# The three convolutions as 64-row by 32-column tiles of the PE array, the upper rows one piece ahead of the lower

## The chip, the core and the metric

The program runs on one core of a Trainium2 chip. The metric is the device time of one execution in microseconds (us). Three timed runs of the kernel before gave 4041.86 us as median (4040.77 to 4042.82). The engines are TensorE (PE, with its weight loads as PEld), VectorE (DVE), ScalarE (ACT), GpSimd (POOL) and SyncE (SP, here only a DMA queue).

## The reference

An image batch x of 64 x 16 channels x 128 x 128 goes through four layers, each "normalise in 8 groups of 2 channels, then transform, then add".

```python
x = x + L0(_gn(x), 5)      # Newton-Schulz inverse of each 128x128 plane, 5 iterations
x = x + L1(_gn(x), ...)    # quantised 3x3 convolution, 16 -> 16 channels, zero padding
x = x + L2(_gn(x), w)      # 5x5 convolution whose kernel is filter_w on its diagonal only
x = x + L3(_gn(x), w)      # 3x3 convolution with circular padding (given as FFTs)
```

The change touches the three convolutions L1, L2 and L3 alone.

## The kernel before

**Two stages.** The first computes layer 0 for all 64 images and ends at about 2274 us. The second runs the convolutions. An image lies in SBUF as 128 partitions = 8 image rows x 16 channels, and 16 blocks j of 8 image rows in the free dimension, each padded to 132 columns. A "piece" is 4 blocks of one image in one layer: one PSUM bank of 128 x 512. There are four pieces (u = 0 to 3) for each image and layer, and 6 banks go round among the pieces (`B_RING`).

**The matmuls of a piece.** Within a block, the 3x3 convolutions (layers 1 and 3) are three 128 x 128 matmuls of 512 columns, one for each horizontal tap, whose weights hold the vertical taps as bands. The image rows just outside a block (one above, one below) are copied by DMA into a tile `xh` of 96 partitions (`halo_copies`, six DMAs an image and layer), and one matmul more with `wth` adds them. Layer 1 has one product; layers 2 and 3 split data and weights into high and low f16 halves and take three products. So a piece of layer 1 has 4 matmuls and one of layer 3 has 12 (`conv`). For layer 2 the tile `xk` holds the image with each of its 8 image rows skewed by one more column (`skew_row`, eight DMAs an image), so that a tap on the diagonal is one fixed offset. `diagonals` uses weight tiles of 128 rows x 32 columns: four of them, at the four column strips of the array, read four different offsets. A product is 8 matmuls (two for each strip) and 4 for the rows outside the block, which only the first and last strip have: 36 a piece.

**The order of the work.** It is written out by hand, in steps s. A step holds layer 1 of image s, layer 2 of image s-1 and layer 3 of image s-3 on TensorE, and the normalisation of layers 2 (image s) and 3 (image s-2) on the other engines. TensorE's order in a step is four pieces of layer 1, `mean(3)`, layer 3 with `var(3)` after its first piece, `mean(2)` after its second and `var(2)` after its fourth, then four pieces of layer 2. `mean` and `var` are tiny f32 matmuls that sum statistics over partitions: `mean(l)` waits for VectorE's `whole_stats`, `var(l)` for its `deviations`, and VectorE's `variance` waits for `var`.

VectorE's order is: layer 1's four `residual`s (PSUM times scale plus the old image), each with the statistics for layer 2 (`chunk_stats`), `deviations(3)` before the fourth; `whole_stats(2)`, `variance(3)`, `clamp`, `normalise(3)`, `integers`; layer 3's four residuals with `deviations(2)`, `variance(2)` and `normalise(2)` between and behind them; layer 2's four residuals, each with statistics; `whole_stats(3)`.

ScalarE has `upper(l)` (two passes that scale the image, `F`, and round it to f16, `xn`), which waits for `normalise(l)`; POOL has `lower(l)`, the low f16 half in four instructions, which waits for `upper`. `wrap` on ScalarE writes layer 3's circular borders. SP issues the skews once `lower(2)` is done, the load of a later image, its share of the halo copies and the store of the result. ScalarE issues the other halo copies in its own queue.

## Time and profile before

| | |
|---|---|
| timed runs, median (lowest to highest) | 4041.86 us (4040.77 to 4042.82) |
| the profiled execution: its time, its span | 4042.99 us, 4041.2 us |
| mean granted clock of TensorE | 0.989 |
| busy: PE, PEld | 3882.1 us (96%), 2994.3 us (74%) |
| busy: DVE, ACT, POOL | 3161.3 us (78%), 2458.9 us (61%), 2416.6 us (60%) |
| instructions | 91064 |
| DMA, whole span | 422.11 MB, mean 104 GB/s |

The page is one profiled execution. Busy time is the union of an engine's instructions; matmuls are pipelined, so that each lasts longer in the record than it holds the array, and the distance between starts is the better measure of their price. "Idle before" is time in which the engine stood still ahead of a group, with what ended it behind the arrow. The granted clock is given as a share of 2.4 GHz: 1.00 is 2.4 GHz and 0.50 is 1.2 GHz. A DMA "lands" when its data are written and its semaphore is up.

### The profile page before, as it was taken

The page shows a single profiled execution, that of the slowest core. Times are in us where ns is not written, and L with a number is a line of the kernel's source. Part 1 is how long each engine was busy: PE and PEld are TensorE (multiplying, and loading weights), DVE is VectorE, ACT ScalarE, POOL GpSimd, SP SyncE. Part 2 cuts the span into 40 slices and gives each one's busy share as a digit, 9 for nine tenths or more (in the row PEclk, how much of TensorE's full clock was granted, in tenths as well). Part 3 has the DMA queues.
Part 4 walks back from the last instruction along what each step waited for, and adds up shares of the span by engine and source line. Part 5 has one row for each costly group of instructions (what it writes and reads, how often), then busy time and mean ns, then how long its engine had stood idle before and what let it go on. Part 6 is the DMA issues. An engine that isn't in the chain of part 4 may idle for free. (4 is left out here: it accounts for less than half of the span.)

```text
span 4041.2 us, 91064 instructions
## 1 busy us (share of the span) xinstructions
PE 3882.1 (96%) x35017; PEld 2994.3 (74%) x35017; DVE 3161.3 (78%) x7205; ACT 2458.9 (61%) x4490; POOL 2416.6 (60%) x3154
## 2 busy tenths in 40 slices
PE   7999999999999999999999589999999999999998
PEld 7999999999999999999999344444444444444443
DVE  5888888888888888888888667777777777777774
ACT  5776677777777777777777345455455455555552
POOL 6888888888888888888888323333332332332332
PEclk9999999999999999999999799999999999999999
DMA  2122211222122222221221368777777777778774
GB/s 71 56 63 64 64 59 59 64 64 59 58 64 64 64 64 64 64 64 56 61 64 43 75 133 175 174 165 162 164 168 175 169 160 163 169 171 175 162 159 106
DMA packets 339918, 422.11 MB, mean 104 GB/s; under 512 B 25312, under 2 KB 288160, under 8 KB 323104
## 3 DMA queue, kind: packets, MB, share of 16 engines
q1 hardware_dynamic: 324128, 377.40, 39.1%
q10 hardware_dynamic: 15360, 38.88, 3.7%
q8 instruction: 282, 4.62, 0.5%
q14 instruction: 148, 1.21, 0.1%
HBM read 135.18 MB, written 134.22 MB: 67 GB/s over the span
## 5 line engine op out<-in xcount | busy, mean ns | idle before, releaser
L1228 POOL TENSOR_TENSOR xn<-F,xn 128x512 f16<-128x512 f32 x512 | 543.4, 1093 | 1189.6 <-ACT xn L1270 1189.6
L1444 PE MATMUL bank<-xn,wt 128*128 128x512 f16 (+1 forms) x3072 | 765.0, 384 | 15.3 <-DVE xn L1314 11.8
L484 ACT ACTIVATE P<-bank 128x512 f32<-128x512 f32 x1024 | 606.6, 608 | 267.6 <-PE bank L1007 155.4
L1466 PE MATMUL bank<-xk,wt 128*32 128x512 f16 x6144 | 634.9, 386 | 43.3 <-DMA xk<-xn 42.9
L1328 DVE SCALAR_TENSOR_TENSOR x<-bank,wu,x 128x512 f32<-128x512 f32 x512 | 377.4, 747 | 299.7 <-PE bank L1471 269.9
L1444 PEld LDWEIGHTS bank<-xn,wt 128*128 128x128 f16 (+1 forms) x3072 | 296.0, 102 | 361.8 <-issue 40.1
L1267 ACT ACTIVATE F<-x,nb,r 128x2048 f32<-128x2048 f32 x128 | 268.1, 2095 | 346.6 <-issue 218.6
L1471 PE MATMUL bank<-xk,wth 128*32 128x512 f16 x3072 | 469.2, 381 | 0.0
L1466 PEld LDWEIGHTS bank<-xk,wt 128*32 128x32 f16 x6144 | 295.6, 95 | 204.9 <-DMA xk<-xn 47.6
L334 POOL TENSOR_TENSOR W<-W 128x512 f16<-128x512 f32 x256 | 289.5, 1160 | 145.1 <-ACT W L517 145.1
L1338 DVE BATCH_NORM_STATS2 bs<-x 128x6 f32<-128x512 f32 x512 | 355.5, 694 | 17.6
L597 DVE BATCH_NORM_STATS2 st<-X 128x6 f32<-128x256 f32 x1024 | 351.5, 409 | 5.8 <-DMA X<-in_x 5.7
L526 ACT ACTIVATE W<-X,nb,r 128x256 f32<-128x256 f32 x512 | 258.7, 587 | 133.8 <-POOL nb L362 130.4
L379 POOL TENSOR_TENSOR S<-P 128x512 f32<-128x512 f32 x256 | 317.8, 1278 | 33.5 <-ACT P L484 33.4
L390 POOL TENSOR_TENSOR P<-P,idt 128x512 f32<-128x512 f32 x256 | 318.3, 1272 | 31.4 <-ACT P L484 31.4
L374 POOL TENSOR_TENSOR YX<-idt,YX 128x512 f32<-128x512 f32 x256 | 323.7, 1275 | 5.5 <-ACT YX L474 5.5
L385 POOL TENSOR_TENSOR S<-S,P 128x512 f32<-128x512 f32 x256 | 318.5, 1277 | 0.0
L1449 PE MATMUL bank<-xh,wth 96*128 96x512 f16 (+1 forms) x1024 | 307.7, 381 | 7.4 <-DMA xh<-xn 7.4
L1471 PEld LDWEIGHTS bank<-xk,wth 128*32 128x32 f16 x3072 | 165.3, 96 | 171.2 <-issue 3.2
L474 ACT ACTIVATE YX<-bank,cs 128x128 f32<-128x128 f32 x1024 | 277.8, 382 | 11.3 <-PE bank L939 2.7
L701 DVE SCALAR_TENSOR_TENSOR X<-bank,cout,X 128x128 f32<-128x128 f32 x1024 | 270.5, 343 | 13.0 <-PE bank L1033 13.0
L635 DVE TENSOR_TENSOR P<-bank,idt 128x512 f32<-128x512 f32 x256 | 176.9, 691 | 109.1 <-PE bank L1024 103.4
(144 smaller groups left out, 8369.3 us busy)
## 6 DMA issues: line engine op xcount, KB each, us to landing
xk<-xn SPq DMA_DIRECT2D x512, 131.8 KB, 4.4
X<-in_x SPq DMA_DIRECT2D x64, 1024.0 KB, 4.8
x_scratch<-X SPq DMA_DIRECT2D x64, 1024.0 KB, 5.8
X<-x_scratch SPq DMA_DIRECT2D x64, 1024.0 KB, 8.6
out<-x SPq DMA_DIRECT2D x64, 1024.0 KB, 6.8
xh<-xn SPq DMA_DIRECT2D x192, 131.8 KB, 4.6
xh<-xn ACTq DMA_DIRECT2D x192, 131.8 KB, 5.5
xh<-xn SPq DMA_DIRECT2D x192, 65.9 KB, 5.2
```

The costliest lines, as they stand in the source:

```text
L374: nc.gpsimd.tensor_tensor(e, eyes, e, ALU.subtract).then_inc(a_new, 1)
L379: nc.gpsimd.tensor_tensor(quad(S, q), quad(P1, q), quad(P2, q), ALU.add).then_inc(s_new, 1)
L385: nc.gpsimd.tensor_tensor(quad(S, q), quad(S, q), quad(P3, q), ALU.add).then_inc(q_new, 1)
L390: nc.gpsimd.tensor_tensor(quad(P2, q), quad(P2, q), eyes, ALU.add).then_inc(r_new, 1)
L484: nc.scalar.activation(into[:, 4 * q:4 * q + 4, :], banks[q][:, :].rearrange("p (m w) -> p m w", m=4), ACT.Copy).then_inc(sb, 1)
L597: ins = nc.vector.bn_stats((st0, st1)[k][:, g, :], group_of(X[slot], g))
L1228: ins = nc.gpsimd.tensor_tensor(padded(xn[l][n % 2], 1)[:, a + 1:a + 5, L:L + H], F[l][:, a:a + 4, :], padded(xn[l][n % 2], 0)[:, a + 1:a ...
L1328: nc.vector.scalar_tensor_tensor(out=dst, in0=bank, scalar=col[:, 0:1], in1=xs_of(l, n)[:, at, :], op0=ALU.mult, op1=ALU.add).then_inc(eva ...
L1338: nc.vector.bn_stats(bst_[l][:, u, :], xs_of(l, n)[:, 4 * u:4 * u + 4, :]).then_inc(gchain[l], 1)
L1444: nc.tensor.matmul(bank, wt[l][:, a, k, :], v, start=(k == a == b == 0), stop=False)
L1466: nc.tensor.matmul(bank[32 * q:32 * q + 32, :], wt[2][:, a, e, 32 * q:32 * q + 32], rows(b, 2 * q + e, 0), start=(a == b == e == 0), stop= ...
L1471: ins = nc.tensor.matmul(bank[32 * q:32 * q + 32, :], wth[2][:, a, e, 32 * q:32 * q + 32], rows(b, 2 * q + e, back), start=False, stop=(a ...
```

## The change

**Tiles.** `conv` and `diagonals` are replaced by one function, `strips`. It issues, for one half of the array's rows (partitions 0 to 63, or 64 to 127) and one unit i of the piece (a product and a weight matrix), four matmuls with 64 x 32 weights, one for each column strip of 32. A piece is 3 units in layer 1, 6 in layer 2 and 9 in layer 3, each once for the upper and once for the lower half: 24, 48 and 72 matmuls of 512 columns.

**The rows outside a block.** In the upper half (image rows 0 to 3) the last strip, output rows 6 and 7 of a block, has no neighbour in its own block; it reads the next block instead, whose first row lies just below. In the lower half (image rows 4 to 7) the first strip, output rows 0 and 1, reads the previous block. `wth` now holds weights for these strips in the shape of `wt`. The tiles `xh`, the halo DMAs on SP and on ScalarE, and their semaphores are gone.

**Order.** The upper half of a piece is issued interleaved unit by unit with the lower half of an earlier piece (`piece`, `lower_strips`), so that the two halves write different banks at a time. The lower half of a piece starts after its upper half's last matmul (`upper_ps`), at the soonest two units into the next piece (`GAP`), and stays at most two pieces behind (`BEHIND`). `conv_ps`, for which VectorE waits, rises with the lower half's last matmul. `mean`, and `var` at two places, first bring the lower halves that they depend on up to date (`finish`). `var(2)` moves from after the fourth piece of layer 3 to after the first piece of layer 2.

**Queues.** ScalarE runs `root(2)` and `upper(2)` before `wrap`, instead of behind it and its DMAs. SP sends each skew as two: the high part as soon as `upper(2)` is done (`high`), the low part after `lower(2)` (`normed`): 16 DMAs of half the size, behind the load and the store of the step. At the start, 18 small weight DMAs stand for 8 earlier ones, and two more tiles are zeroed.

```diff
-                    def conv(l, n, u):
...
-                                nc.tensor.matmul(bank, wt[l][:, a, k, :], v, start=(k == a == b == 0), stop=False)
-                        if u == 0:
-                            pe.wait_ge(halo[l][n % 2], 16 * 6 * (n // 2 + 1))
...
+                    def strips(l, n, u, half, i):
+                        a, b = products[l][i // mats[l]]
+                        k = i % mats[l]
+                        if half == 0 and i == 0:
+                            if u == 0:
+                                ready(l, n)
+                            bank_free(l, n, u)
+                        bank = bank_of(l, n, u)
+                        part = slice(64 * half, 64 * half + 64)
+                        for q in range(4):
+                            back = {(1, 0): -1, (0, 3): 1}.get((half, q), 0)
+                            cols_ = slice(32 * q, 32 * q + 32)
+                            w = (wth if back else wt)[l][part, a, k, cols_]
+                            if l == 2:
+                                at = (4 * u + 1) * PW + L + SK - (2 * q + k) + back * (PW + RB)
+                                v = xk[n % 2][part, b, at:at + 4 * PW].rearrange("p (j w) -> p j w", w=PW)[:, :, 0:H]
+                            else:
+                                at = 4 * u + 1 + back
+                                v = padded(xn[l][n % 2], b)[part, at:at + 4, L + k - 1:L + k - 1 + H]
+                            ins = nc.tensor.matmul(bank[cols_, :], w, v, start=(half == i == 0),
+                                                   stop=(half == 1 and i == length[l] - 1))
+                        if half == 1 and i == length[l] - 1:
+                            ins.then_inc(conv_ps[l], 1)
+                        if half == 0 and i == length[l] - 1:
+                            ins.then_inc(upper_ps, 1)
...
                     def mean(l, n):
+                        finish(l - 1, n, BPI - 1)
...
+                    def lower_strips():
+                        k, i = below
+                        if i == 0:
+                            pe.wait_ge(upper_ps, k + 1)
+                        strips(*order[k], 1, i)
+                        below[:] = [k, i + 1] if i + 1 < length[order[k][0]] else [k + 1, 0]
+                    def piece(l, n, u):
+                        k = place[l, n, u]
+                        for i in range(length[l]):
+                            strips(l, n, u, 0, i)
+                            if below[0] < k - (i < GAP):
+                                lower_strips()
+                        while below[0] < k - BEHIND:
+                            lower_strips()
...
-                    sp.wait_ge(normed[1], 1)
-                    halo_copies(sp, 1, 0, False)
+                    def skew(n, part):
+                        for r in range(RB):
+                            at, to = PW + L, PW + L + SK - r
+                            sp.dma_start(xk[n % 2][C * r:C * r + C, part, to:to + RUN],
+                                         xn[2][n % 2][C * r:C * r + C, part, at:at + RUN]).then_inc(skewed[n % 2], 16)
...
-                            sp.wait_ge(wrapped, 2 * (s - 1))
-                            halo_copies(sp, 3, s - 2, False)
+                        if there(s):
+                            need(sp, conv_ps[2], BPI * (s - 1))
+                            sp.wait_ge(high[2], s + 1)
+                            skew(s, 0)
+                            sp.wait_ge(normed[2], s + 1)
+                            skew(s, 1)
```

**TensorE, the end of a step.** Before, from `mean(2)` on (`s,gm` and `q,gm` are the two statistics matmuls):

```order
L1478 MATMUL bank<-s,gm 128x1 [waits gvar_sb2,bst_done2]
L1444 MATMUL bank<-xn_1,wt 128x512 [waits evac1]
L1444 MATMUL bank<-xn_1,wt 128x512 x8
L1449 MATMUL bank<-xh_1,wth 128x512 x3
L1444 MATMUL bank<-xn_1,wt 128x512 [waits evac1]
L1444 MATMUL bank<-xn_1,wt 128x512 x8
L1449 MATMUL bank<-xh_1,wth 128x512 x3
L1483 MATMUL bank<-q,gm 128x1 [waits spread2]
L1466 MATMUL bank<-xk,wt 32x512 [waits evac1,halo2_1]
L1466 MATMUL bank<-xk,wt 32x512 x7
L1471 MATMUL bank<-xk,wth 32x512 x4
```

In the change, the first units of layer 2's first piece (`xk`, upper half) with those of layer 3's third piece (`xn_0`, lower half), where the wait for the skews now stands:

```order
L1445 MATMUL bank<-xk,wt 32x512 [waits evac1,skewed0]
L1445 MATMUL bank<-xk,wt 32x512 x2
L1445 MATMUL bank<-xk,wth 32x512
L1445 MATMUL bank<-xn_0,wth 32x512
L1445 MATMUL bank<-xn_0,wt 32x512 x3
L1445 MATMUL bank<-xk,wt 32x512 x3
L1445 MATMUL bank<-xk,wth 32x512
```

And the end of that piece:

```order
L1445 MATMUL bank<-xk,wt 32x512 x3
L1445 MATMUL bank<-xk,wth 32x512
L1445 MATMUL bank<-xn_0,wth 32x512
L1445 MATMUL bank<-xn_0,wt 32x512 x3
L1461 MATMUL bank<-q,gm 128x1 [waits spread2]
L1445 MATMUL bank<-xk,wt 32x512 [waits evac1]
```

The matmul for `var(2)` (`q,gm`) stood ahead of the first matmul that waits for the skews; it now stands behind six units that follow this wait, and so do the lower halves of layer 3's last pieces.

**ScalarE, from `root(2)` on.** Before (`sd` is the square root, `T` belongs to the next step):

```order
L1275 ACTIVATE sd<-ve 128x1 [waits gvar_sb2]
L1249 ACTIVATE xn_0<-xn_0 128x2x16 [waits normed3]
L1251 ACTIVATE xn_0<-xn_0 128x2x16
L1253 ACTIVATE xn_0<-xn_0 128x2x132 [waits wrap_chain]
L1254 ACTIVATE xn_0<-xn_0 128x2x132
L1184 DMA xh_0<-xn_0 16x2x2108 [waits wrapped]
L1184 DMA xh_0<-xn_0 16x2x2108 x2
L1267 ACTIVATE F<-x_0,nb,r 128x2048 [waits normed2,scale_set2]
L1270 ACTIVATE xn_0<-F 128x16x128 [waits scaled_f2]
```

In the change:

```order
L1265 ACTIVATE sd<-ve 128x1 [waits gvar_sb2]
L1257 ACTIVATE F<-x_0,nb,r 128x2048 [waits normed2,scale_set2]
L1260 ACTIVATE xn_0<-F 128x16x128 [waits scaled_f2]
L1239 ACTIVATE xn_0<-xn_0 128x2x16 [waits normed3]
L1241 ACTIVATE xn_0<-xn_0 128x2x16
L1243 ACTIVATE xn_0<-xn_0 128x2x132 [waits wrap_chain]
L1244 ACTIVATE xn_0<-xn_0 128x2x132
L1250 ACTIVATE T<-X,ncol,acol 128x2048 [waits normed1,x1_in0]
```

The two passes of `upper(2)` now stand right behind the square root; the wait for `normed3` and the DMAs that stood ahead of them are behind them or gone.

## Rows read from the trace of the kernel before

**Rows 1.** The page: busy time, share and instructions by engine; clock in 40 slices.

```profile
PE 3882.1 (96%) x35017; PEld 2994.3 (74%) x35017; DVE 3161.3 (78%) x7205; ACT 2458.9 (61%) x4490; POOL 2416.6 (60%) x3154
...
PEclk9999999999999999999999799999999999999999
```

**Rows 2.** Stretches, 3000 to 3500 us: busy time and instructions by engine, clock, DMA.

```profile
3000.00:3500.00 500.00, 481.81 (x4092) 229.85 (x4092) 376.40 (x871) 254.57 (x228) 159.55 (x151) 1.00 0.76 168
```

**Rows 3.** Groups by line, 2600 to 4000 us: count, busy, mean ns, idle before.

```profile
L1228 POOL TENSOR_TENSOR xn<-F,xn 128x512 f16<-128x512 f32 x424 | 448.4, 1089 | 950.4 <-ACT xn L1270 950.4
...
L1328 DVE SCALAR_TENSOR_TENSOR x<-bank,wu,x 128x512 f32<-128x512 f32 x424 | 312.4, 747 | 221.6 <-PE bank L1471 214.9 <-PE bank L1449 4.9
```

**Rows 4.** Timeline of TensorE in one step: start us, us, instructions.

```profile
3304.60 0.62 PE L1466 MATMUL bank<-xk,wt 128*32 128x512 f16 x8 [0.16 <-DMA xk<-xn]
...
3307.22 0.62 PE L1466 MATMUL bank<-xk,wt 128*32 128x512 f16 x6
...
3315.17 0.83 PE L1444 MATMUL bank<-xn,wt 128*128 128x512 bf16 x3
...
3316.06 0.82 PE L1444 MATMUL bank<-xn,wt 128*128 128x512 bf16 x3
...
3322.13 2.13 PE L1444 MATMUL bank<-xn,wt 128*128 128x512 f16 x9
...
3324.75 0.28 PE L1478 MATMUL bank<-s,gm 128*128 128x1 f32 x2
```

**Rows 5.** Timeline of 3304.60 to 3304.62 us, after TensorE's wait.

```profile
3304.60 0.11 PEld L1466 LDWEIGHTS bank<-xk,wt 128*32 128x32 f16 x6 [0.24 <-DMA xk<-xn]
3304.60 0.40 PE L1466 MATMUL bank<-xk,wt 128*32 128x512 f16 x4 [0.16 <-DMA xk<-xn]
```

**Rows 6.** Timeline of VectorE in one step.

```profile
3304.48 0.16 DVE L1364 TENSOR_SCALAR ve<-bank 128x1 f32<-128x1 f32 x1 [0.91 <-PE bank L1483]
...
3305.92 0.16 DVE L1372 RECIPROCAL ra<-sd 128x1 f32<-128x1 f32 x1 [0.62 <-ACT sd L1275]
...
3306.86 0.21 DVE L1381 TENSOR_SCALAR nb<-r,m 128x1 f32<-128x1 f32 x1
...
3316.87 0.75 DVE L1328 SCALAR_TENSOR_TENSOR x<-bank,sws,X 128x512 f32<-128x512 f32 x1
...
3318.26 0.73 DVE L1328 SCALAR_TENSOR_TENSOR x<-bank,sws,X 128x512 f32<-128x512 f32 x1
...
3321.02 0.14 DVE L1350 TENSOR_TENSOR dv<-bs,bank 128x8 f32<-128x8 f32 x1
...
3321.75 0.74 DVE L1328 SCALAR_TENSOR_TENSOR x<-bank,sws,X 128x512 f32<-128x512 f32 x1
```

**Rows 7.** The chain of waits in the same step: start us, us, what.

```profile
3313.06 2.10 ACT F L1267
...
3317.18 4.24 POOL xn L1228 x4
...
3321.43 0.59 SPq L1176
...
3326.19 5.11 DMA xk<-xn
...
3331.35 0.83 PE bank L1466 x8
```

**Rows 8.** Tile xk, 2600 to 4000 us: the DMAs' time to landing.

```profile
DMA to landing us min/median/max: 3.3/4.4/5.7
```

**Rows 9.** Timeline of TensorE near the end: a wait and what follows.

```profile
3977.86 0.38 PE L1478 MATMUL bank<-s,gm 128*128 128x1 f32 x2 [1.77 <-DVE s L1342]
3978.11 3.11 PE L1444 MATMUL bank<-xn,wt 128*128 128x512 f16 x9
```

**Rows 10.** Two stretches there: before the clock fell, and while it was down.

```profile
3974.00:3979.00 5.00, 3.23 (x33) 1.48 (x28) 3.25 (x8) 3.02 (x2) 1.87 (x2) 1.00 0.24 56
3979.10:3982.40 3.30, 3.30 (x11) 1.35 (x9) 1.36 (x3) 0.00 (x0) 2.26 (x3) 0.50 0.02 5
```

More of the change, by code:

```diff
@@ L136, in conv_net @@
         w_loaded = sem("w_loaded")
-        W_PIECES = 3 + 2 + len(HALO2)
+        W_PIECES = 3 + sum(len(edges[l]) for l in (1, 2, 3))
         w_top = sem("w_top")
@@ L1117, in conv_net @@
             T = sb("T", [H, NJ, H])
-            xh = [None] + [None if l == 2 else [sb(f"xh{l}_{n}", [6 * C, parts[l], NJ * PW], kinds[l]) for n in range(2)]
-                           for l in (1, 2, 3)]
             xk = [sb(f"xk{n}", [H, 2, SFLAT], f16) for n in range(2)]
@@ L1141, in conv_net @@
             wrap_chain = sem("wrap_chain")
-            halo = [None] + [[sem(f"halo{l}_{n}") for n in range(2)] for l in (1, 2, 3)]
-            skewed = halo[2]
+            skewed = [sem(f"skewed{n}") for n in range(2)]
             xk_zeroed = sem("xk_zeroed")
+            upper_ps = sem("upper_ps")
             conv_ps = [None] + [sem(f"conv_ps{l}") for l in (1, 2, 3)]
@@ L1154, in conv_net @@
             CH = 8
+            GAP = BEHIND = 2
             LATE = (None, 0, 1, 3)
@@ L1168, in conv_net @@
             place = {piece: k for k, piece in enumerate(order)}
+            products = (None, [(0, 0)], [(0, 0), (0, 1), (1, 0)], [(0, 0), (0, 1), (1, 0)])
+            length = [None] + [len(products[l]) * mats[l] for l in (1, 2, 3)]
             def bank_of(l, n, u):
                 return banks[place[l, n, u] % B_RING]
[L1173 to L1185 removed]
             with nc.Block() as block:
@@ L1296, in _ @@
                             root(2, s)
+                            upper(2, s)
                         if there(s - 2):
                             wrap(s - 2)
[L1299 to L1302 removed]
                 @block.vector
@@ L1484, in var, with finish @@
                                          stop=True).then_inc(gvar[l], 1)
+                    below = [0, 0]
+                    def lower_strips():
[12 more added lines that the diff above has]
+                            lower_strips()
+                    def finish(l, n, u):
+                        k = place[l, n, u]
+                        while below[0] <= k:
+                            lower_strips()
                     for s in range(STEPS):
-                        if there(s):
-                            for u in range(BPI):
-                                conv(1, s, u)
+                        for u in range(BPI):
+                            if there(s):
+                                piece(1, s, u)
                         if there(s - 2):
@@ L1493, in _ @@
                             if there(s - 3):
-                                conv(3, s - 3, u)
+                                piece(3, s - 3, u)
                             if there(s - 2) and u == 0:
+                                if there(s):
+                                    finish(1, s, BPI - 2)
                                 var(3, s - 2)
-                            if there(s):
-                                if u == 1:
-                                    mean(2, s)
-                                if u == 3:
-                                    var(2, s)
-                        if there(s - 1):
-                            for u in range(BPI):
-                                diagonals(s - 1, u)
+                            if there(s) and u == 1:
+                                mean(2, s)
+                        for u in range(BPI):
+                            if there(s - 1):
+                                piece(2, s - 1, u)
+                            if there(s) and u == 0:
+                                if there(s - 3):
+                                    finish(3, s - 3, 0)
+                                var(2, s)
+                    finish(*order[-1])
 def kernel(x, L1_conv_weight_int8, L1_conv_scale_weight, L1_conv_bias, L2_conv_filter_w, L3_conv_weight):
```

101 lines of the change are left out of this document (26 added, 75 removed).

## The prediction, made before the change was run

> **What bounds the kernel now.** First the page: TensorE is busy 96% of the span, and its clock is at full speed but for two places, the change of stage and the end [rows 1]. The change touches only the second stage. There the table of stretches shows TensorE busy 481.8 of 500 us against VectorE's 376.4, ScalarE's 254.6 and POOL's 159.6, with the DMA engines at 0.76 [rows 2]. The length of a step comes from a count: POOL's L1228 runs 8 times a step and 424 times in 1400 us [rows 3], so 53 steps of 26.4 us. VectorE has 376.4 / 500 x 26.4 = 19.9 us of work in each, and its residuals stand idle behind TensorE's L1471 for most of their 222 us [rows 3]. So TensorE sets the time.
>
> The timeline of a step gives its parts [rows 4]. Layer 2's first piece starts at 3304.60 and its second at 3307.22: 2.62 us for 36 tiles of 128 x 32, of which four (or two) run side by side, in 12 rounds: 0.218 us a round. Layer 1 takes 3316.06 - 3315.17 = 0.89 us for 4 matmuls, layer 3 3324.75 - 3322.13 = 2.62 us for 12. Four pieces of each are 24.5 us; the four small statistics matmul pairs at 0.28 add 1.1, waits the last 0.8.
>
> **TensorE's work after.** A unit is four tiles of 64 rows. If the upper and the lower half run beside each other, a round of eight tiles should hold the array as long as one of four does, 0.218 us. The units are 4 x (3 + 6 + 9) = 72 a step for each half; the written order leaves about one unpaired (in `finish` ahead of `var(3)` and with `GAP`), so 73 rounds: 15.9 us, and 17.0 with the small matmuls, against 25.6. The trace of before has no 64-row tile, so this 0.218 is the first unknown. Its lower bound is the same 0.218, since each tile still streams 512 columns. For the upper bound there are two ways. One is that the halves take turns: 144 rounds of 0.218. The other is the rate at which pairs of weight load and matmul are fed: eight are wanted in 0.218 us, 27 ns each, and before shows no steady rate above four in 0.218, 54 ns, which would make a round 0.435. For the lower value speaks that behind a wait four matmuls and six weight loads start within 20 ns, and that the six loads together take 0.11 us [rows 5]: loads of different strips overlap, and the feed is quick at least for a burst. I take 0.218.
>
> The Trainium skill ("TensorE: Matmul & The Clock Gate", "Wait — 56ns, not 53.3ns?") has two floors. With decoding in firmware a matmul costs about 62 ns, by which a round would be 0.50 us; the trace disagrees, since four tiles go in 0.218. Otherwise starts are never under about 25 ns apart, by which a round would be 0.20 and the 0.218 stand; no row here shows a long stream that tests it, nor whether the weight load counts towards it.
>
> **What then sets the step.** With 9 us of TensorE's work gone, I look for loops that come back to the same instruction a step later. I start the clock where TensorE begins layer 2's first piece.
>
> *Up to normalise(2), common to both loops.* The lower half of layer 3's last piece ends with the 11th unit from there: 2.4 us, and 0.4 for the length of a matmul [rows 5]. Its residual of 0.75 [rows 3] brings 3.5. `var(2)`, issued after six rounds at 1.3 us, is no later: its matmul pair takes 0.28 [rows 4], and from VectorE's `ve` to the reciprocal are 3305.92 - 3304.48 = 1.44 us [rows 6], in all 3.0. `normalise(2)` takes from 3305.92 to 3307.07: 1.15 us [rows 6]. With 0.1 of semaphores it ends at 4.8 us. Before, `var(2)` did not depend on the skews; now it does, and that closes loop 1.
>
> *Loop 1, by the DMAs.* ScalarE's two passes take 3317.18 - 3313.06 = 4.1 us to POOL's start [rows 7]; they no longer wait for `wrap` and three DMA issues (ScalarE had `nb` at 3307.07 [rows 6] and began at 3313.06, a delay of 6.0 us that goes). At 9.0 us SP may issue. It has 16 DMAs in place of 8. Eight take 0.68 us each ((3326.19 - 3321.43) / 7 [rows 7]). POOL's 4.24 us [rows 7] lie under the first eight, so halving hides POOL but doubles the issues: the last is issued 15 x 0.68 = 10.2 us later, at 19.2. It lands 3.3 to 5.7 us after that, median 4.4 at the full size [rows 8]. With half the bytes and no halo copies in the way I take 3.9: 23.1 us to the next start. Ends: 15 x 0.59 (a single issue [rows 7]) and 3.3 give 21.2; 0.68 and 5.7 give 24.9.
>
> *Loop 2, by VectorE.* After `normalise(2)` come layer 2's four residuals with statistics, 3318.26 - 3316.87 = 1.39 us each [rows 6]: 5.6, so at 10.4 `whole_stats(3)` and `mean(3)`. Then three of layer 1's (4.2) and `deviations(3)` (3321.75 - 3321.02 = 0.73 [rows 6]) at 15.4, `var(3)` at 15.7. TensorE has 27 rounds of layer 3 behind it, 5.9 us, and `mean(2)` 0.3: 21.9 us. In this loop TensorE stands still for about 2.2 us ahead of `mean(3)` and 2.6 ahead of `var(3)`.
>
> *The clock.* After a stop of 1.77 us with TensorE otherwise busy (3.23 of 5.00 us) its clock was at 0.50 for the next 3.3 us [rows 9, 10], 1.2 in place of 2.4 GHz; nine matmuls took 3.11 us [rows 9] where they take 2.13 [rows 4]. The change has two such stops a step. A stretch at 0.50 costs half of its 3.3 us, 1.7, if it falls on the 27 rounds of loop 2: 23.6 us. It costs nothing where it falls ahead of `var(3)`, since that stop shortens. So loop 2 lies between 21.9 and, with two such stretches, 25.2.
>
> VectorE's own work, 19.9, is under both. The larger of 23.1 and 23.6 is my step: 26.4 - 23.6 = 2.8 us a step. I count 62 steps (61 hold all three layers; the three that fill and the three that drain the pipeline together count as one): 174 us.
>
> **The edits that I cost at nothing.** Halo copies gone: their wait never held TensorE in the steady part; the issue time on ScalarE is counted above. Two more POOL memsets and 10 more small DMAs at the start lie ahead of the first work of POOL and beside the first images; if uncovered, some 5 us. Layer 2's later residuals follow TensorE at 1.3 us a piece and VectorE at 1.39, so VectorE is not held. `wrap` behind `upper(2)` ends near 10.4 us, just ahead of layer 3 at 10.8; if it came late, some tenths of a us a step. The waits for `upper_ps` come three units after the matmul that raises it.
>
> **The sum.** The profiled execution took 4042.99 us, 1.1 above the median of the runs. 4043.0 - 174 = 3869, and as a median 3868 us.
>
> **The rivals.**
> *Fed too slowly* (slower). The place is TensorE's stream of 584 tiles a step. From (26.4 - 1.1 - 0.8) / 584 = 42 ns a pair it decides against the change; at the 54 ns that before proves, a step is 73 x 0.435 + 1.1 = 32.9 us: 6.5 x 62 = 403 more, 4445 us. For it: nothing longer than a burst is shown faster. Against: rows 5. Chance 0.19.
> *The halves take turns* (slower; the change doesn't do what it says). 144 x 0.218 + 1.1 = 32.5 us: 4420 us. Against it: column strips do run side by side; no row tells of row halves. Chance 0.05.
> The Trainium skill ("TensorE: Matmul & The Clock Gate", "Measured speedup vs the span model") has 16 tiles of 32 x 32 with 512 columns in 660 ns. By that, halves run together; no run here shows it yet.
> *Long landings or a clock that stays low* (less gain). Steps of 25.2 us: 1.2 x 62 = 74, 3967 us. For it: two stops a step, 5.7 us landings; against: the clock came back at once in rows 9 and 10 once TensorE was busy. Chance 0.17.
> *No clock loss and short landings* (more gain): loop 2 alone, 21.9 us: 4.5 x 62 = 279, 3763 us. Chance 0.13.
> *The gain is used up exactly*: feeding at about 42 ns. Chance 0.03.
>
> **How the numbers follow.** The forecast keeps 0.43; its own range is steps of 22.8 to 24.5 us, 3820 to 3925 us. Faster by over 0.2% (8 us, what a measurement of this kernel can tell) are the forecast and the two rivals on its side, 0.73; within it 0.03; slower 0.24. The range reaches from 3750, a little below the best loop, to 4250, into the cases between 42 and 54 ns; about 0.2 is left out, nearly all above.
>
> **What would show it.** A round: layer 3's eight tiles should start every 0.22 us; 0.4 or more means a rival on TensorE. TensorE busy time in the second stage should fall clearly below 96%, with idle time ahead of the two statistics matmuls that wait for VectorE and ahead of the first matmul on `xk` that waits for DMA. SP should issue 16 skews in about 10 us. The granted clock should show a half-speed stretch in many steps. The step between two starts of POOL's `lower(2)` should be 23 to 24.5 us. I am wrong if the step is 26 us or more, or if TensorE has no idle time left.

## The result, and the profile after the change

| | before, run beside it | after |
|---|---|---|
| timed runs, median (lowest to highest) | 4042.34 us (4040.77 to 4043.26, 4 runs) | 3918.71 us (3896.02 to 3921.51, 4 runs) |
| ratio of after to before, 95% interval | | 0.9682 [0.9646, 0.9719] |
| the profiled execution: its time, its span | 4042.99 us, 4041.2 us | 3920.5 us, 3918.7 us |
| mean granted clock of TensorE | 0.989 | 0.949 |

The change makes the kernel 3.2% faster. The forecast was 3868 us, with 3820 to 3925 for its own case: the direction and the case came out, the gain was 71% of the one foretold.

The page of the kernel after: busy time by engine, the clock in 40 slices, the queue of instruction packets (packets, MB, share), and the DMA issues with their time to landing.

```profile
PE 3571.3 (91%) x58569; PEld 2914.9 (74%) x58569; DVE 3148.7 (80%) x7205; ACT 2450.6 (63%) x4490; POOL 2419.3 (62%) x3156
...
PEclk9999999999999999999999969889889888889988
...
q8 instruction: 465, 7.62, 0.8%
...
xk<-xn SPq DMA_DIRECT2D x1024, 65.9 KB, 2.4
```

Against [rows 1], TensorE has 23552 more matmuls and is busy 311 us less. The clock, which stood at 9 in every slice of the second stage, now shows an 8 in eleven of its 16 slices. The skews land in 2.4 us in place of 4.4 [rows 8]. Queue `q8`, which carries instructions, moves 465 packets, against 282 packets and 4.62 MB before; the last part of this section comes back to it.

A stretch of the second stage of the kernel after, in the columns of [rows 2] (busy PE, PEld, DVE, ACT, POOL; clock; DMA share; GB/s), and the group of POOL's `lower` in it.

```profile
2500.00:3800.00 1300.00, 1076.99 (x30518) 564.35 (x30526) 1036.52 (x2417) 700.15 (x629) 444.11 (x420) 0.90 0.56 131
```

```profile
L1218 POOL TENSOR_TENSOR xn<-F,xn 128x512 f16<-128x512 f32 x420 | 444.6, 1091 | 851.4 <-ACT xn L1260 851.4
```

TensorE's share fell from 96% to 83%, VectorE's rose from 75% to 80%. At 8 a step, the 420 instructions are 52.5 steps in 1300 us: a step is 24.75 us, against 26.4 [rows 3]. The clock of 0.90 is a mean of two levels, 1.00 and 0.50, so 20% of the time, 5.0 us of each step, is at half speed.

**The rounds.** Timeline of TensorE inside a piece of layer 2: start us, us, instructions.

```profile
3311.00 0.48 PE L1445 MATMUL bank<-xk,wt 64*32 64x512 f16 x6
...
3311.22 0.49 PE L1445 MATMUL bank<-xk,wt 64*32 64x512 f16 x6
...
3311.44 0.49 PE L1445 MATMUL bank<-xk,wt 64*32 64x512 f16 x6
```

Six of a round's eight matmuls stand in each row, the other two in rows left out between. A round starts every 0.22 us. Over stretches of 64 to 128 pairs of weight load and matmul the starts are 27.1 ns apart on the average, 0.217 us a round: the 0.218 of the forecast. The Trainium skill ("TensorE: Matmul & The Clock Gate", "Measured speedup vs the span model") has small tiles of different rows and columns at work together; this trace agrees, with four column strips in each of two row halves.

**The step by loop 1.** The chain of waits of the kernel after, from the residual of layer 3's last piece to the same residual a step later.

```profile
3310.05 0.75 DVE x L1314
...
3311.91 2.11 ACT F L1257
...
3314.04 1.92 ACT xn L1260
...
3316.02 0.51 SPq L1193
...
3320.38 1.43 SPq L1193
...
3325.65 0.72 SPq L1193
3326.37 0.04 issue
3326.41 3.57 DMA xk<-xn
...
3330.03 1.51 PE bank L1445 x47
...
3333.14 0.75 DVE x L1314
```

It takes 23.09 us; 23.1 were forecast. In this chain the issue of the DMA that is waited for stands as part of its DMA row: 15 rows of L1193 and then the sixteenth, which starts at 3326.41, 10.4 us after the first. One of the 16 takes 1.43 us where most take 0.59. The data land 3.6 us after the sixteenth issue starts.

**The step by loop 2.** The next step in the same chain.

```profile
3340.60 0.76 DVE x L1314
...
3345.40 0.17 DVE q L1346
...
3345.62 0.59 PE bank L1461 x2
...
3346.20 3.55 PE bank L1445 x47
...
3350.07 5.39 PE bank L1445 x171
...
3357.21 0.84 issue
3358.05 3.69 PE bank L1445 x125
3361.74 1.70 issue
```

Here the way goes by VectorE's `deviations(3)` (`q`) to `var(3)` (L1461), and then through TensorE's own work, with two stops marked "issue" in it. (The counts behind the x are those of the chain's pieces, not of all matmuls.) In the piece at 3346.20 a round takes 0.43 us: rounds of eight start at 3346.54, 3346.96 and 3347.39. That is twice the 0.217 of full speed. TensorE's stops from there on, and the clock of the two stretches:

```profile
3340.74 0.38 PE L1456 MATMUL bank<-s,gm 128*128 128x1 f32 x2 [1.77 <-DVE s L1328]
...
3345.62 0.59 PE L1461 MATMUL bank<-q,gm 128*128 128x1 f32 x2 [1.73 <-DVE q L1346]
```

```profile
3342.40:3349.20 6.80, 5.07 (x94) 2.62 (x82) 6.42 (x19) 0.20 (x1) 0.94 (x1) 0.50 0.60 94
3349.30:3373.00 23.70, 17.55 (x567) 9.30 (x556) 17.49 (x39) 13.22 (x11) 8.47 (x8) 1.00 0.59 137
```

The first stop ends at 3340.74 and the clock falls at 3342.4, before the second stop begins. It is at 0.50 for 6.8 us, through the second stop and into layer 3. Over 2500 to 3700 us the chain holds nine passes through the skews, some 17% of the time; the other steps go by loop 2.

Waits of TensorE of 2500 to 3800 us in the kernel after: us in total, times, longest us.

```profile
PE bank L1461 <- DVE q L1346: 95.9, 53, 2.7
PE bank L1456 <- DVE s L1328: 73.8, 51, 1.8
PE bank L1445 <- issue: 43.3, 39, 2.2
...
PE bank L1445 <- DMA xk<-xn: 9.9, 9, 2.2
```

Each step has a stop of 1.8 us ahead of `var(3)` and one of 1.4 ahead of `mean(3)`; nine steps have one ahead of layer 2's first matmul, for the DMAs. The 39 put down to "issue", 1.1 us each, were in no step of the forecast, and the kernel before has no such row. Twenty of them begin 1 to 5 us after layer 2's first matmul, the other 19 begin 8 to 10 us after it. They are not waits for VectorE: in the longest one both engines stand still, VectorE for TensorE. Timelines of both engines there, and the DMA packets of the 0.2 us from 2597.3 on, in which it began:

```profile
2599.61 0.39 PE L1445 MATMUL bank<-xk,wt 64*32 64x512 f16 x3 [2.25 <-issue]
```

```profile
2600.04 0.75 DVE L1314 SCALAR_TENSOR_TENSOR x<-bank,wu,x 128x512 f32<-128x512 f32 x1 [2.20 <-PE bank L1445]
```

```profile
q8 instruction: 1, 0.02, 27.7%
```

No semaphore ends these stops, but the packets of queue `q8` fit all of them. A packet has 16,384 bytes, and in these 1300 us TensorE runs 61044 matmuls and weight loads for 240 packets, 254 for each. The kernel before has nearly the same quotient (21216 for 84, or 253), and so does experiment 1 (255): the queue carries TensorE's instructions. In the trace's packet records all 39 stops end 2.15 to 2.58 us after the start of a packet; the one above started at 2597.39. Of TensorE's 113 stops that a semaphore ends, only 15 lie between 2.1 and 2.6 us behind one. Take a running balance, 256 instructions for each packet less those that TensorE has run, with its slow drift taken out. It is low there: at the start of these 39 packets it is 43 to 173 instructions below its mean, while at the other 201 its median is 26 above. So TensorE runs out of instructions and waits for the next packet. Why a packet comes so late isn't shown.

Taken from one first matmul of layer 2 to the next, 46 steps of 2538 to 3678 us last 22.3 to 28.1 us, 24.8 on the average. The 14 of them with more than 1.2 us of "issue" stops last 26.6 us; the other 32 last 24.0.

### The profile page after: what moved, and what is told of

Its sections match the earlier page's. It is cut to its first block and busy times, and to the rows that moved or that the text cites. A ratio compares the mean times of both kernels' runs of the same rounds, so it can differ in the third digit from the quotient of the medians.

```text
span 3918.7 us, 137986 instructions
## 1 busy us (share of the span) xinstructions
PE 3571.3 (91%) x58569; PEld 2914.9 (74%) x58569; DVE 3148.7 (80%) x7205; ACT 2450.6 (63%) x4490; POOL 2419.3 (62%) x3156
## 5 line engine op out<-in xcount | busy, mean ns | idle before, releaser
L1445 PE MATMUL bank<-xn,wt 64*32 64x512 f16 (+1 forms) x18432 | 1066.1, 430 | 28.0 <-issue 16.1
L1445 PE MATMUL bank<-xn,wth 64*32 64x512 f16 (+1 forms) x6144 | 1050.2, 429 | 7.9 <-issue 7.9
L1445 PEld LDWEIGHTS bank<-xn,wt 64*32 64x32 f16 (+1 forms) x18432 | 462.3, 100 | 256.5 <-issue 122.7
L1445 PE MATMUL bank<-xk,wt 64*32 64x512 f16 x9216 | 533.1, 383 | 39.3 <-issue 21.3
L1445 PE MATMUL bank<-xk,wth 64*32 64x512 f16 x3072 | 525.3, 383 | 8.1 <-issue 8.0
L1445 PEld LDWEIGHTS bank<-xn,wth 64*32 64x32 f16 (+1 forms) x6144 | 395.7, 100 | 100.2 <-issue 10.8
L1445 PEld LDWEIGHTS bank<-xk,wt 64*32 64x32 f16 x9216 | 249.9, 93 | 166.4 <-issue 43.9
L1265 ACT ACTIVATE sd<-ve 128x1 f32<-128x1 f32 x128 | 25.7, 201 | 447.0 <-DVE ve L1350 447.0
```

The lines of the kernel that those rows point to most:

```text
L1445: ins = nc.tensor.matmul(bank[cols_, :], w, v, start=(half == i == 0), stop=(half == 1 and i == length[l] - 1))
```

## The experiments

The kernel before, run beside each batch, had medians of 4039.95 to 4043.25 us.

**1. The halves one after the other.** All upper units of a piece, then all lower units of the piece before it: the same tiles, and only the borders of the blocks run side by side.

```diff
                         for i in range(length[l]):
                             strips(l, n, u, 0, i)
-                            if below[0] < k - (i < GAP):
-                                lower_strips()
-                        while below[0] < k - BEHIND:
+                        while below[0] < k:
                             lower_strips()
```

> The change, but the upper half of a piece is issued whole and then the lower half of the piece before it, so that the two halves of the array run beside each other only at the switches. Theory (the gain comes from halves that run side by side): the written order has 120 rounds of 0.218 us a step in place of 73, so TensorE needs 26.2 + 1.1 us, is busy nearly always again, and the step is about 28 us: some 4140 us. Rival (halves never ran side by side in a way that matters; the gain came from the queues and the dropped halo copies): the time stays near 3920.

Measured: 4192.87 us in one run. A step is 28.9 us (360 `lower(2)` in 1300 us). The stretch, in the columns above:

```profile
2900.00:3400.00 500.00, 458.21 (x10214) 236.56 (x10217) 343.38 (x805) 234.53 (x208) 148.02 (x140) 0.84 0.49 114
```

TensorE is the bound again, 92% busy, at a clock of 0.84. So the gain hangs on the pairing of the halves: without it the rest of the change costs 150 us. That the clock falls here too, with TensorE so busy, stays unexplained; it adds to the length of the step.

**2. Fewer columns.** Every matmul of the three layers streams 384 columns of 512, so that a quarter of the output is left out.

```diff
-                                v = padded(xn[l][n % 2], b)[part, at:at + 4, L + k - 1:L + k - 1 + H]
-                            ins = nc.tensor.matmul(bank[cols_, :], w, v, start=(half == i == 0),
+                                v = padded(xn[l][n % 2], b)[part, at:at + 3, L + k - 1:L + k - 1 + H]
+                            ins = nc.tensor.matmul(bank[cols_, 0:384], w, v, start=(half == i == 0),
```

> The change, with each convolution matmul cut from 512 to 384 columns (a quarter of the output is left out). It asks what holds a round of eight tiles to 0.217 us. If it is the array (512 columns at 2.4 GHz), a round takes 0.163 us and a pair of weight load and matmul 20 ns. If it is the feed of instructions at 27 ns a pair, it stays at 0.217; with a floor of 25 ns a pair it is 0.200. The whole time is of no use here, only the spacing of the starts.

Measured: 3888.12 us in one run. Timeline of TensorE inside a piece of layer 2:

```profile
3292.60 0.35 PE L1445 MATMUL bank<-xk,wt 64*32 64x384 f16 x6
...
3292.77 0.35 PE L1445 MATMUL bank<-xk,wt 64*32 64x384 f16 x6
```

A round now takes 0.163 us, three quarters of 0.217, and pairs start 20.4 ns apart. So at 512 columns the feed of pairs has room, and the time of a round scales with the columns. The rival "fed too slowly", by the pair, falls for good. Over longer times the supply does matter: the "issue" stops grow from 43.3 us in 39 times to 127.0 us in 89, and 83 of the 89 end 2.16 to 2.57 us after the start of a packet on `q8`. The second lesson is the time: with a quarter of TensorE's streaming gone the kernel is 0.8% faster. That isn't a clean measure of what the streaming is worth, since the longer stops and a clock of 0.84 in place of 0.90 took back a part of it.

**3. The queues alone.** The kernel before with the change's order on ScalarE (`upper(2)` ahead of `wrap`) and the skews by halves on SP, but with its own matmuls and halo copies.

```diff
+                        if there(s):
+                            need(sp, conv_ps[2], BPI * (s - 1))
+                            sp.wait_ge(high[2], s + 1)
+                            for r in range(RB):
+                                skew_row(sp, r, s, 0)
                         if there(s - 2):
                             sp.wait_ge(wrapped, 2 * (s - 1))
                             halo_copies(sp, 3, s - 2, False)
+                        if there(s):
+                            sp.wait_ge(normed[2], s + 1)
+                            for r in range(RB):
+                                skew_row(sp, r, s, 1)
```

> The kernel before, with the change's queues alone: upper(2) ahead of wrap on ScalarE, skews in two halves behind the load and the store on SP; matmuls, order on TensorE and halo copies as before. Theory (TensorE bound the kernel before): the step can fall from 26.4 us to TensorE's 25.6 at the best, so 3990 to 4042 us. Rival (the queues gave the gain): about 3920.

Measured: 4259.53 us (4256.52 to 4262.24), ratio 1.0533 [1.0517, 1.0549]; a step is 29.7 us. Neither theory foresaw it. The chain of waits in one step:

```profile
3311.15 2.11 ACT F L1272
...
3322.14 0.52 SPq L1176
...
3322.72 0.63 SPq L1184
...
3324.05 4.91 DMA xh<-xn
...
3329.01 0.82 PE bank L1453 x3
```

Layer 3's halo copies (L1184) now stand behind `upper(2)`, `wrap` and eight half skews (L1176), and land when TensorE has long come to layer 3's first piece. With 142.5 us in 43 waits over 1300 us they hold it back 3.3 us each time. So the new order on ScalarE and SP is no gain in itself; it can be had only because the other part of the change takes the halo copies away. The forecast counted the end of the halo copies as nothing. That holds in the old order and not in the new one.

**4. The stops filled.** Six idle matmuls of 128 x 128 weights and 510 columns ahead of `mean(3)`, seven ahead of `var(3)`, into a bank of their own; only the clock should notice.

```diff
+                    def fill(s, count):
+                        need(pe, gvar_sb[2], s)
+                        for _ in range(count):
+                            nc.tensor.matmul(banks[6][:, 2:512], wt[3][:, 0, 0, :], ..., start=True, stop=True)
...
                         if there(s - 2):
+                            if there(s):
+                                fill(s, 6)
                             mean(3, s - 2)
...
                                     finish(1, s, BPI - 2)
+                                    fill(s, 7)
                                 var(3, s - 2)
```

> The change, with idle matmuls (128 x 128, 510 columns, into an unused part of a bank) ahead of the two statistics matmuls of layer 3 at which TensorE stops: 6 ahead of mean(3), 7 ahead of var(3), 1.3 and 1.5 us where the mean stops are 1.5 and 1.8. Theory (the clock costs what the forecast missed: 5.1 us at half speed in a step of 24.75, and 22.9 without): the granted clock is near 1.0 in the second stage, the step about 23 us, 3805 to 3840 us. Rival (the stops are the effect of other loops and the clock costs nothing on the path): 3920 or, as the filling delays the statistics, up to 1 us a step more, 3980.

Measured: 3843.87 us (3834.17 to 3851.74), ratio 0.9512 [0.9496, 0.9528]. The stretch:

```profile
2500.00:3800.00 1300.00, 1187.11 (x33026) 609.54 (x33014) 1079.47 (x2534) 731.52 (x663) 469.54 (x444) 0.99 0.58 137
```

With 13 more matmuls a step the kernel is 1.9% faster. The clock is 0.99, the step 23.4 us (444 in 1300 us). So the stops cost by the clock: 4.5 us a step less at half speed gave 1.35 us back. The time is just above the expected 3805 to 3840. Over 2500 to 3700 us the chain now passes through the skews 27 times in 51 steps, against nine times in the change: loop 1 sets about half of the steps. Of 50 steps the 20 without an "issue" stop last 23.0 us, loop 1's figure; the 13 with more than 1.2 us of them, 1.9 in the mean, last 24.2.

**5. The statistics later.** `mean(3)` after layer 3's first piece, `var(3)` after its second, which gives VectorE more time.

```diff
-                        if there(s - 2):
-                            mean(3, s - 2)
                         for u in range(BPI):
                             if there(s - 3):
                                 piece(3, s - 3, u)
                             if there(s - 2) and u == 0:
+                                mean(3, s - 2)
+                            if there(s - 2) and u == 1:
```

> The change, with mean(3) issued after layer 3's first piece and var(3) after its second (in the change: ahead of the first, and after the first). Theory (loop 2 runs through var(3) and the rounds behind it; the stops there bring the clock down): 18 rounds in place of 27 stand behind var(3), loop 2 is 19.9 us, the stops nearly vanish, the clock stays near 1.0, and loop 1, the skews, sets a step of 22.5 to 23.1 us: 3775 to 3815 us. Rival (VectorE and the normalisation of layer 3 are then late and take the gain): 3880 or more.

Measured: 3859.26 us (3855.21 to 3870.20), 0.9557 [0.9541, 0.9572], a step of 23.6 us, clock 0.94. A gain of 1.5%, but less than expected: the stops shrink to 1.2 and 0.9 us and don't go, and the skews' issues rise to 17% of the chain. A third stop appears as well. With `mean(3)` behind it, layer 3's first piece now comes sooner, and 36 times in 1300 us TensorE stands still ahead of it, 43.8 us in all. Each of these stops ends 0.10 us after the last pass of ScalarE's `wrap`, for which this piece waits. The profile puts them down to "issue" too.

**6 to 9. The skews on two queues.** In 6, SP issues the first eight and three of the low half, ScalarE the other five behind `wrap`. 7 adds the order of 5, 8 the filler of 4 (with the order of after). 9 is 7 with ScalarE's `quotients(s + 1)` (`T`) ahead of its five issues.

```diff
-                            skew(s, 1)
+                            skew(sp, s, 1, range(3))
...
                             wrap(s - 2)
+                        if there(s):
+                            need(act, conv_ps[2], BPI * (s - 1))
+                            act.wait_ge(normed[2], s + 1)
+                            skew(act, s, 1, range(3, RB))
```

> The change, with the low half of each skew issued by two queues: three rows by SP and five by ScalarE, behind wrap. SP's last issue then comes about 3 us sooner. Theory (loop 1 at 23.1 us sets some steps, loop 2 with a clock of 0.9 the others): a small gain, 3860 to 3915 us, and the stops ahead of the first matmul on xk go. Rival (the skews never hold the step): 3919 or, by ScalarE's issue time, later.

> Both of the last two. Theory: with loop 1 near 20 us and loop 2 near 20 us, VectorE's 20 us of work set the step, 20.5 to 21.5 us: 3670 to 3740 us. Rival (only one of the loops counts): no better than the better of the two alone.

> The skews shared by two queues and the idle matmuls that keep the clock up (6 ahead of mean(3), 7 ahead of var(3)). Theory: loop 2 at full clock, 21.9 us and what the filling delays: a step of 22 to 22.5 us, 3750 to 3780 us. Rival (with the filling alone 3844 was already loop 2, not loop 1): no change against the filling alone.

Measured: 6: 3891.76 us (3881.42 to 3899.15), 0.9631 [0.9613, 0.9649]. 7: 3857.52 us (3852.56 to 3857.95), 0.9545 [0.9531, 0.9560]. 8: 3853.08 us (3847.97 to 3855.13), 0.9535 [0.9519, 0.9550]. In 6 TensorE no longer waits for the DMAs of `xk`, and the gain is what was expected. But 7 is no better than 5 and 8 no better than 4: both expectations failed, by over 100 and by over 70 us. The chain of waits of 7 shows a loop that nobody had counted:

```profile
3201.80 4.24 POOL xn L1219 x4
...
3206.11 0.51 ACTq L1180
...
3209.32 2.10 ACT T L1251
...
3211.45 1.23 DVE T L1300
...
3213.77 2.11 ACT F L1258
...
3217.72 1.99 ACT X L1272
...
3221.04 2.11 ACT F L1258
...
3225.16 4.24 POOL xn L1219 x4
```

From POOL to POOL it is 23.4 us: `lower(2)`, five issues in ScalarE's queue, and only then `T`, VectorE's clamp and `normalise(3)`, layer 3's passes on ScalarE, layer 2's, and POOL again. ScalarE, 57% busy in these steps, looked free. The same loop holds up TensorE through `wrap`, whose last pass is L1245. Waits of TensorE over 2500 to 3700 us in 7:

```profile
PE bank L1450 <- ACT xn L1245: 94.6, 43, 2.7
```

> The later statistics and the shared skews, with ScalarE's quotients (the pass that writes T) ahead of its skew issues instead of behind them. In the run without this the chain of waits went through ScalarE alone: POOL, five DMA issues, T, VectorE's clamp and normalise(3), four passes, normalise(2), 23.4 us a step. Theory (that loop took the gain): it opens, and VectorE's 20 us of work or the skews at about 20.5 set the step: 21 to 22 us, 3690 to 3750 us. Rival (a step of 23.5 is set by something that none of these edits touches): 3840 to 3860 again.

```diff
                             quotients(s + 1)
+                        if there(s - 1):
+                            need(act, conv_ps[2], BPI * (s - 2))
+                            act.wait_ge(normed[2], s)
+                            skew(act, s - 1, 1, range(3, RB))
```

Measured: 3801.88 us (3797.13 to 3804.31), 0.9411 [0.9395, 0.9426]; a step is 22.6 us. The five issues moved behind one pass of ScalarE give 1.4% against 7, so the loop through ScalarE held it, at least in part. It stays short of the expected time: the clock is 0.95, and the stops ahead of `mean(3)` and `var(3)` are still there (63.5 us in 53 and 36.2 us in 50 times, over 1200 us). The waits for `wrap` are there too: 40 stops of 1.2 us that the profile puts down to "issue" end 0.10 us after its last pass, besides five that it names.

**10. `var(2)` first.** `var(2)` back ahead of layer 2's first piece, so that it doesn't depend on the skews.

```diff
+                        if there(s):
+                            if there(s - 3):
+                                finish(3, s - 3, 0)
+                            var(2, s)
                         for u in range(BPI):
                             if there(s - 1):
                                 piece(2, s - 1, u)
-                            if there(s) and u == 0:
-                                if there(s - 3):
-                                    finish(3, s - 3, 0)
-                                var(2, s)
```

> The change, with var(2) ahead of layer 2's first piece, as it stood before. Theory (normalise(2) waits for layer 3's last residual, whose matmuls still stand behind the wait for the skews, so var(2) is not the last to come): 3919 us within 0.5%. Rival (the moved var(2) is what closes the loop): a step shorter by a few tenths of a us at least, under 3895 us.

Measured: 3921.44 us (3916.65 to 3931.70), 0.9708 [0.9689, 0.9726]: no difference from the change that can be measured. The lower half of layer 3's last piece still runs beside layer 2's first, behind the wait for the skews, and its residual closes the loop.

**11. Whole skews.** Eight DMAs of full size after `lower(2)`, in place of 16 halves.

```diff
-                            sp.wait_ge(high[2], s + 1)
-                            skew(s, 0)
                             sp.wait_ge(normed[2], s + 1)
-                            skew(s, 1)
+                            skew(s, slice(0, 2))
```

> The change, with each skew sent as one DMA of both halves after lower(2), 8 issues in place of 16. Theory (loop 1): the last issue comes 9.0 + 4.2 + 7 x 0.68 = 18.0 us from the start of layer 2, against 19.2, and lands in 3.3 to 4.4 us against 2.4 to 3.6: within 0.6 us a step of the change either way, 3885 to 3945 us. Rival (halving is what makes the skews early enough): slower by POOL's 4.2 us in the steps that the skews set, 4000 us or more.

Measured: 3936.44 us (3931.82 to 3950.71), 0.9748 [0.9727, 0.9768], 0.5% above the change, with an interval that just parts from its own. Whole skews land in 4.4 us as before, halves in 2.4. The halving is a small gain: it hides POOL and shortens the landing, and gives most of it back in eight more issues.

**12. The parts together.** 9 with four idle matmuls ahead of `mean(3)` and three ahead of `var(3)`.

```diff
                             if there(s - 2) and u == 0:
+                                if there(s):
+                                    fill(s, 4)
                                 mean(3, s - 2)
                             if there(s - 2) and u == 1:
                                 if there(s):
                                     finish(1, s, BPI - 2)
+                                    fill(s, 3)
                                 var(3, s - 2)
```

> The last combination (later statistics, shared skews, T first), which took 3802 us with the clock at 0.95 in the second stage and steps of 22.6 us, with 4 idle matmuls ahead of mean(3) and 3 ahead of var(3). Theory (what is left above VectorE's 20 us is half-speed stretches on the path): the clock goes to about 1.0 and the step to 21.2 to 22 us, 3715 to 3765 us. Rival (the clock no longer counts, since VectorE sets most steps): 3790 to 3830, the filling being in the way.

Measured: 3786.97 us (3781.57 to 3788.97), 0.9368 [0.9352, 0.9383], the fastest version. The stretch:

```profile
2500.00:3700.00 1200.00, 1060.08 (x31483) 578.45 (x31475) 1037.23 (x2447) 707.53 (x639) 450.84 (x427) 1.00 0.57 144
```

The clock is full and the step 22.5 us (427 in 1200 us), but the filler gives only 0.4% here, where it gave 1.9% in experiment 4. Of 52 steps 42 hold more than 1.2 us of "issue" stops, 2.0 in the mean, and last 22.8 us; the ten with less last 21.7. With steps of 21.7 throughout, the time would be some 50 us lower (0.8 x 62) and within what was expected. That this is near the 21.9 of the forecast's loop 2 means nothing: only 18 rounds stand behind `var(3)` here, and the same sum gives 19.9.

The stops have two causes. ScalarE and TensorE in one of them:

```profile
2664.71 0.41 ACT L1245 ACTIVATE xn<-xn 128x264 f16<-128x264 f16 x1
```

```profile
2665.21 0.40 PE L1450 MATMUL bank<-xn,wt 64*32 64x512 f16 x3 [1.30 <-issue]
```

`wrap` ends at 2665.11 (the row's 2664.71 and 0.41 are rounded), and layer 3's first piece starts 0.10 us later. Of the 95 "issue" stops in 1200 us, 93.7 us in all, 35 are of this kind, 36.8 us. The other 60 are the wait for instructions: 54 end 2.15 to 2.60 us after the start of a packet on `q8`, six 2.9 to 3.4 us after. No run has tried either cure, `wrap` ahead of `upper(2)` again or the same work in fewer, larger matmuls.

## Why the prediction was right, and where its sizes were off

**The round was right.** 0.218 us was taken for eight tiles, 0.217 measured. Experiments 1 and 2 exclude both rivals on TensorE: the halves run together, and a pair of weight load and matmul can start every 20.4 ns. The argument from the burst [rows 5] held for stretches of 64 to 128 pairs, which is up to one packet of 256 instructions. Beyond that it didn't hold: the rival was right that the feed can run short, and wrong about the place, which is the packets and not the single pair. The Trainium skill ("TensorE: Matmul & The Clock Gate", "Wait — 56ns, not 53.3ns?") says that starts are never under about 25 ns apart; with 512 columns this could not be told, with 384 the trace disagrees.

**Loop 1 was right as a sum**: 23.1 forecast, 23.09 in the chain. Its parts are close too: the last issue starts 10.4 us after the first, for 10.2, and lands 3.6 us after its start, for 3.9. Over 51 steps the sixteenth issue starts 9.7 to 12.0 us after the first (median 10.6) and lands in 2.4 to 4.3 us (2.7). That most issues take 0.59 us and a few over 1.4 was not foreseen; the rate taken from before, 0.68, covers both. Of what closes it the forecast said that `var(2)` "now does" depend on the skews. It does, but experiment 10 shows that nothing hangs on it; the forecast's own figures, 3.5 us for the residual and 3.0 for `var(2)`, already said so.

**Loop 2 was mis-sized, in two terms.** The first is "one half-speed stretch", 3.3 us long and 1.7 in price, on top of 21.9. It was taken from the one place of before where the clock fell [rows 9, 10]. Here a second stop follows 5 us after the first. Measured are 5.0 us a step at half speed, though the two stops by themselves are shorter than forecast (1.4 and 1.8 us for 2.2 and 2.6). Steps without further stops last 24.0 us for 23.6. That this is so near is in part luck: with the clock kept up they last 23.0 (experiment 4), so the clock costs 1.0 us of them and not 1.7, and the rest stands at 23.0 and not at 21.9. Loop 1 then sets about half of the steps; whether loop 2 by itself would reach 21.9 isn't shown. The second term was missing: the stops in which TensorE waits for instructions, some 0.8 us a step, which bring the mean to 24.8. Experiment 4 shows how the two work together: with the clock kept up, steps without such stops fall from 24.0 to 23.0 us and those with many from 26.6 to 24.2. So 1.9 us of such stops cost 1.2 us at full clock. In the change 2.1 us of them cost 2.6, and the steps that hold them have 6.1 us at half speed, the others 4.7: there a stop costs clock as well.

The change has far more instructions for TensorE, 117138 matmuls and loads in all against 70034, and the 183 packets more on `q8` hold just these (47104 instructions, 257 a packet). The forecast counted tiles only by their time in the array. That the stops are waits for these packets is read from the trace; no run changed the number of instructions with the rest held, and why some packets come late is open.

**The sum.** The step by the count of `lower(2)` was 24.75 us, 1.15 more than forecast, over 62 steps 71 us. The forecast missed by 51. The other 20 came from the two ends. Of the 122.5 us between the two profiled executions, 101 lie in the last 61 of the 63 steps between the first `lower(2)` and the last (1.66 each), 11 in the first two, 4.4 ahead of them and 6.1 behind the last. For filling and draining together the forecast had counted one step, 2.8 us; they gave 21.5. Two errors of unlike sign, then, and not one small one: that the total came out within 51 us is in part luck.

**The edits counted at nothing.** VectorE was not held, as said: 19.7 us of work in a step of 24.75. `wrap` was just in time, as said: no stop of TensorE in the change ends with it. It is late as soon as the step gets shorter (experiments 5, 7, 9 and 12). The halving of the skews was rightly taken as a near balance (0.5%). The end of the halo copies was not free in the sense of the text: without it the new order of the queues costs 5.3% (experiment 3).

## What to carry to other kernels

When the engine that bounds a kernel gets a third of its work taken off, the new time isn't set by the next busy engine but by loops that come back to the same instruction a step later; write each of them down with its queue issues and landings, those through half-idle engines too. Short stops of TensorE that fall several times in a step can cost by themselves and by the clock, and a few idle matmuls in them can pay. Smaller tiles mean more instructions: a stop that the profile puts down to "issue" is to be held against the packets of the instruction queue, and against waits that the profile may have failed to name. A reorder is worth what still stands behind the moved wait, so try it apart from the part that clears the queue.

## What the runs showed of the hardware that was not expected

- TensorE stood still for 0.2 to 2.3 us in 39 places of 1300 us where no semaphore held it and VectorE waited for it in the longest; before has none of these. All 39 end 2.15 to 2.58 us after the start of a 16,384-byte packet on the instruction queue, of which there is one for every 254 matmuls and weight loads.
- After a stop of 1.77 us TensorE's clock was at half for 6.8 us, through a second stop of 1.73 us; thirteen idle matmuls a step brought the granted clock of the stage from 0.90 to 0.99.
- A stream of weight load and matmul on 64 x 32 tiles keeps up one pair every 20.4 ns for 384 columns and every 27.1 ns for 512, over 64 to 128 pairs.
- SP's issue of a skew takes 0.59 us for 66 KB and 0.62 for 132 KB (medians); what the size changes is the landing, 2.4 against 4.4 us. An issue at times takes more than twice as long (1.43 us in the chain above).
